# Cross-attention: the per-head merge as four transposes, the maximum row copied by ScalarE, the maximum tiles in another order

## The reference, cut to what matters

```
q = qdq(layernorm(x)) @ qdq(wq).T + bq          # 256 x 512
k, v = split(ctx @ wkv.T + bkv)                 # 4096 x 512 each
attn = softmax(q_h @ k_h.T / sqrt(32))          # for each of 16 heads: 256 x 4096
o_h  = attn @ v_h                               # 256 x 32
out  = qdq(concat(o_h)) @ qdq(wp).T + bp        # qdq: int8 rounding with a scale per row
```

## Time and profile before

| | us |
|---|---|
| three timed runs | 626.0, 627.62, 627.74 |
| median | 627.62 |
| the profiled execution | 625.34 |
| its span, first to last instruction | 623.5 |
| granted TensorE clock, mean | 0.997 of full speed |

### The profile page before, as it was taken

One profiled execution on the slowest core, in us unless ns is written; L12 is line 12 of the kernel. 1 busy time (PEld: TensorE's weight loads), 2 busy tenths in 40 slices (PEclk: granted clock), 3 DMA queues, 4 the chain that ended last, 5 costly groups with the idle time before them and its releaser, 6 DMA issues.

```text
span 623.5 us, 12623 instructions
## 1 busy us (share of the span) xinstructions
PE 603.5 (97%) x4455; PEld 482.0 (77%) x4456; DVE 369.4 (59%) x680; ACT 299.1 (48%) x424; POOL 228.4 (37%) x120
## 2 busy tenths in 40 slices
PE   8999999999999999999999999999899899999997
PEld 6877788888887677776777777776798789789996
DVE  3996530430434778887788788874764244376562
ACT  4444233233232555555555555555247678644451
POOL 2000200000002778887887888881100664410000
PEclk9999999999999999999999999999999899999999
DMA  8873644615639655556666555620032315145510
GB/s 292 310 238 121 188 171 160 202 67 161 208 102 280 172 152 151 147 155 158 159 158 157 147 147 147 157 83 2 1 136 69 136 67 202 69 159 199 187 63 34
DMA packets 29758, 92.19 MB, mean 148 GB/s; under 512 B 5472, under 2 KB 9568, under 8 KB 23008
## 3 DMA queue, kind: packets, MB, share of 16 engines
q1 hardware_dynamic: 28480, 89.67, 47.3%
q10 hardware_dynamic: 1248, 2.10, 0.9%
HBM read 65.02 MB, written 18.35 MB: 134 GB/s over the span
## 4 chain that ended last, share of the span: by engine, by line
PE 88%; DVE 4%; ACT 4%; issue 2%; POOL 1%; DMA 1%; POOLq 0%; SPq 0%; ACTq 0%; DVEq 0%
PE ps L340 16%; PE ps L341 16%; PE ps L342 16%; PE ps L1291 11%; PE ps L1388 10%; PE ps L1400 9%; PE ps L1414 4%; POOL p_sum L581 1%; PE ps L1374 1%; PE ps L1376 1%; ACT h_ring L772 1%; DMA f_ring<-stream 1%; PE ps L1273 1%; ACT probs L744 1%; PE ps L1364 1%
## 5 line engine op out<-in xcount | busy, mean ns | idle before, releaser
L700 ACT ACTIVATE p_ring<-ps 128x1024 f32<-128x1024 f32 x128 | 125.7, 1022 | 100.7 <-PE ps L1388 68.2
L961 DVE TENSOR_REDUCE m_part<-ps 128x1 f32<-128x512 f32 x240 | 150.5, 685 | 29.1 <-PE ps L1291 26.1
L581 POOL TENSOR_TENSOR p_sum<-p_sum,p_ring 128x1024 f32<-128x1024 f32 x60 | 142.8, 2380 | 9.1 <-ACT p_ring L700 4.8
L1291 PE MATMUL ps<-k_stack,q_max 96*128 96x512 f32 x240 | 86.7, 421 | 0.9 <-issue 0.6
L1388 PE MATMUL ps<-q_stack,k_stack 98*128 98x256 f32 x512 | 80.7, 286 | 0.2 <-ACT p_ring L700 0.2
L1388 PEld LDWEIGHTS ps<-q_stack,k_stack 98*128 98x128 f32 x512 | 74.8, 189 | 7.7 <-ACT p_ring L700 1.3
L1400 PE MATMUL ps<-p_ring,v_head 128*32 128x256 f32 x1024 | 71.6, 383 | 0.1
L1291 PEld LDWEIGHTS ps<-k_stack,q_max 96*128 96x128 f32 x240 | 40.9, 188 | 22.9 <-DVE m_part L961 12.7
L916 DVE SCALAR_TENSOR_TENSOR kl_buf<-ps,biases,kh_buf 128x512 fp32r<-128x512 f32 x32 | 23.6, 748 | 58.1 <-ACT kh_buf L661 57.8
L312 DVE TENSOR_TENSOR l_ring<-f_ring,h_ring 128x2048 fp32r<-128x2048 f32 x22 | 50.2, 2288 | 12.5 <-ACT h_ring L308 12.5
L340 PE MATMUL ps<-xt_h,h_ring 128*128 128x256 f32 x200 | 56.5, 282 | 0.0
(11 more groups left out here) (194 smaller groups left out, 1052.8 us busy)
## 6 DMA issues: line engine op xcount, KB each, us to landing
f_ring<-stream SPq DMA_DIRECT2D x29, 1024.0 KB, 4.9
k_stack<-kh_scratch SPq DMA_DIRECT2D x60, 256.0 KB, 4.6
kh_scratch<-kh_buf SPq DMA_DIRECT2D x32, 256.0 KB, 5.5
kl_scratch<-kl_buf SPq DMA_DIRECT2D x32, 256.0 KB, 5.9
v_head<-v_all SPq DMA_DIRECT2D x16, 512.0 KB, 3.0
k_stack<-kl_scratch SPq DMA_DIRECT2D x30, 256.0 KB, 4.2
v_all<-stream SPq DMA_DIRECT2D x4, 256.0 KB, 4.7
f_ring<-stream SPq DMA_DIRECT2D x4, 256.0 KB, 5.8
```

The lines of the kernel that those rows point to most:

```text
L581: nc.gpsimd.tensor_tensor(p_sum[:, p, :], p_ring[:, 0, :] if n == 0 else p_sum[:, p, :], p_ring[:, c % 4, :], ALU.add).then_inc(sums_done, 1)
L700: nc.scalar.activation(p_ring[:, c % 4, :], ps[:, 2 * (c % 2):2 * (c % 2) + 2, :].rearrange("p b n -> p (b n)"), ACT.Exp, scale=XSCALE).th ...
L961: nc.vector.reduce_max(m_part[:, j // NT, j % NT:j % NT + 1], maximum_bank(j), AX.X).then_inc(max_read, 1)
L1291: nc.tensor.matmul(maximum_bank(j), q_max[p][0:SPLIT_ROWS, at128(j % NT)], k_stack[p][0:SPLIT_ROWS, j // NT * D:(j // NT + 1) * D], start= ...
```

## The change

The merge becomes four fp32 transposes of `o_t` with the identity into bank 5 (numerators in its first half, denominators in the second). VectorE adds the four groups with two `tensor_reduce`, one of 8 denominators into `den`, one of 256 elements in PSUM into 64 elements of the same bank, then divides as before. The merge stands behind s6 and waits for the read of t13; t15 moves to bank 4, t1' waits for the read of t15, and the maximum rows, which use bank 5, wait until the outputs are written. VectorE's normalisation comes behind the negated maxima. ScalarE instead of VectorE copies the maximum row. The output maximum is taken once for heads 0 to 13, then for 14 and for 15. `pick` and its nine instructions on GpSimd go. The order on TensorE in one head, after:

```diff
+        def merge_bank():
+            return bank(5)
         def maximum_bank(j):
-            return bank((6, 4, 6)[j] if j < 3 else 5 if j == 15 else 4 + j % 3)
+            return bank((6, 4, 6)[j] if j < 3 else 4 + j % 3)
 # ScalarE
+            def maximum_row(h, p):
+                act.wait_ge(mrow_done, h + 1)
+                nc.scalar.copy(q_stack[p][SPLIT_ROWS:SPLIT_ROWS + MAX_ROWS, :], maximum_row_bank()).then_inc(mrow_ready, 1)
+            maximum_row(0, 0)
             exponentials(0, first=True)
-            with act.Fori(1, H - 1) as h:
-                exponentials(h)
+            maximum_row(1, 1)
+            with act.Fori(0, H // 2 - 1) as i:
+                exponentials(2 * i + 1)
+                maximum_row(2 * i + 2, 0)
+                exponentials(2 * i + 2)
+                maximum_row(2 * i + 3, 1)
 # VectorE
             def normalize_output(h):
                 dve.wait_ge(merge_done, h + 1)
-                order.step(nc.vector.reciprocal(r_den[:], bank(4).rearrange("p (t c) -> p t c", c=64)[:, 0:NT, DH]))
+                groups = merge_bank().rearrange("p (u g d) -> p u d g", u=2 * NT, d=DH)
+                added = merge_bank()[:, N:N + NT * DH].rearrange("p (t d) -> p t d", t=NT)
+                order.step(nc.vector.tensor_reduce(den[:], groups[:, NT:2 * NT, 0, :], axis=AX.X, op=ALU.add))
+                order.step(nc.vector.tensor_reduce(added, groups[:, 0:NT, :, :], axis=AX.X, op=ALU.add))
+                order.step(nc.vector.reciprocal(r_den[:], den[:]))
...
-                chunk_maxima(h + 1, 3, 15)
+                chunk_maxima(h + 1, 3, 16)
+                negate_maximum(h + 1)
                 if not first:
                     normalize_output(h - 1)
-                chunk_maxima(h + 1, 15, 16)
-                negate_maximum(h + 1)
-                if not first:
-                    output_maximum(h - 1)
                 if after:
-                    chunk_maxima(h + 2, 0, 2)
-                maximum_row(h + 1, 1 - p)
-                if after:
-                    chunk_maxima(h + 2, 2, 3)
+                    chunk_maxima(h + 2, 0, 3)
 # TensorE
             def maximum_rows(h):
                 pe.wait_ge(negm_ready, NT * h + NT)
+                wait(pe, o_done, NT * (h - 1))
...
             def merge(h, last_two=False):
                 pe.wait_ge(ot_evac, h + 1)
                 if not last_two:
-                    pe.wait_ge(max_read, 16 * (h + 2) + 13)
-                for t in range(NT):
-                    nc.tensor.matmul(bank(4)[:, 64 * t:64 * t + DH], o_t[:, at128(t)], pick[:, 0:DH],
-                                     start=True, stop=True)
-                    last = nc.tensor.matmul(bank(4)[:, 64 * t + DH:64 * t + DH + 1], o_t[:, at128(NT + t)],
-                                            pick[:, DH:DH + 1], start=True, stop=True)
+                    pe.wait_ge(max_read, 16 * (h + 2) + 14)
+                else:
+                    pe.wait_ge(o_done, NT * h)
+                for t in range(2 * NT):
+                    last = nc.tensor.transpose(merge_bank()[:, at128(t)], o_t[:, at128(t)], ident[:])
                 last.then_inc(merge_done, 1)
```

More of the change, by code:

```diff
@@ L136, in perceiver @@
         ident_b = sb("ident_b", [P, P], BF16)
-        pick = sb("pick", [P, DH + 1], F32)
         ones_col = sb("ones_col", [P, DH], F32)
@@ L549, in _ @@
             order.step(nc.gpsimd.memset(minus_half[:], -0.5))
-            for tile in (ident, ident_b, pick):
+            for tile in (ident, ident_b):
                 order.step(nc.gpsimd.memset(tile[:], 0.0))
@@ L555, in _ @@
                                         pattern=[[-1, P]], channel_multiplier=1).then_inc(consts_ready, 1)
-            for first in range(0, P, DH):
-                order.step(nc.gpsimd.affine_select(out=pick[:, 0:DH], in_=pick[:, 0:DH], compare_op=ALU.not_equal,
-                                                   fill=1.0, base=-first, pattern=[[-1, DH]], channel_multiplier=1))
-                order.step(nc.gpsimd.affine_select(out=pick[:, DH:DH + 1], in_=pick[:, DH:DH + 1],
-                                                   compare_op=ALU.not_equal, fill=1.0, base=-first,
-                                                   pattern=[[-1, 1]], channel_multiplier=1))
             nc.gpsimd.memset(ones_col[:], 1.0).then_inc(ones_set, 1)
@@ L1002, in normalize_output @@
+                added = merge_bank()[:, N:N + NT * DH].rearrange("p (t d) -> p t d", t=NT)
+                order.step(nc.vector.tensor_reduce(den[:], groups[:, NT:2 * NT, 0, :], axis=AX.X, op=ALU.add))
+                order.step(nc.vector.tensor_reduce(added, groups[:, 0:NT, :, :], axis=AX.X, op=ALU.add))
+                order.step(nc.vector.reciprocal(r_den[:], den[:]))
                 for t in range(NT):
-                    nc.vector.scalar_tensor_tensor(out=o_all[:, t, bass.ts(h, DH)], in0=bank(4)[:, 64 * t:64 * t + DH],
+                    nc.vector.scalar_tensor_tensor(out=o_all[:, t, bass.ts(h, DH)], in0=added[:, t, :],
@@ L1004, in normalize_output, with output_maximum @@
                                                    scalar=r_den[:, t:t + 1], in1=bv_row[:, bass.ts(h, DH)],
                                                    op0=ALU.mult, op1=ALU.add).then_inc(o_done, 1)
-            def output_maximum(h):
-                dve.wait_ge(o_done, NT * h + NT)
-                order.step(nc.vector.tensor_reduce(a_part[:, :, h], o_all[:, :, bass.ts(h, DH)], axis=AX.X,
+            def output_maximum(part, first, last):
+                dve.wait_ge(o_done, NT * last)
+                order.step(nc.vector.tensor_reduce(a_part[:, :, part], o_all[:, :, first * DH:last * DH], axis=AX.X,
@@ L1010, in output_maximum, with head @@
                                                    op=ALU.max, apply_absolute_value=True))
             negate_maximum(0)
-            chunk_maxima(1, 0, 2)
-            maximum_row(0, 0)
-            chunk_maxima(1, 2, 3)
-            def head(h, p, after=True):
+            chunk_maxima(1, 0, 3)
+            def head(h, after=True):
                 first = isinstance(h, int) and h == 0
-                chunk_maxima(h + 1, 3, 15)
+                chunk_maxima(h + 1, 3, 16)
+                negate_maximum(h + 1)
@@ L1034, in _ @@
             with dve.Fori(0, H // 2 - 2) as i:
-                order.enter(4, i, 8)
-                head(2 * i + 1, 1)
-                head(2 * i + 2, 0)
+                order.enter(4, i, 10)
+                head(2 * i + 1)
+                head(2 * i + 2)
                 order.leave(4, H // 2 - 2)
-            head(H - 3, 1)
-            head(H - 2, 0, after=False)
+            head(H - 3)
+            head(H - 2, after=False)
+            output_maximum(0, 0, H - 2)
             def add_last(n):
@@ L1285, in maxima @@
                     elif j == 1:
-                        wait(pe, o_done, NT * (h - 2))
+                        pe.wait_ge(max_read, 16 * h)
                     elif j == 4:
@@ L1362, in maximum_rows @@
                 pe.wait_ge(negm_ready, NT * h + NT)
+                wait(pe, o_done, NT * (h - 1))
                 for t in range(NT):
-                    last = nc.tensor.matmul(bank(5)[SPLIT_ROWS:SPLIT_ROWS + MAX_ROWS, at128(t)], neg_hl[:, t, :],
-                                            ident[:], start=True, stop=True)
+                    last = nc.tensor.matmul(maximum_row_bank()[:, at128(t)], neg_hl[:, t, :], ident[:],
+                                            start=True, stop=True)
                 last.then_inc(mrow_done, 1)
```

33 lines of the change are left out of this document (15 added, 18 removed).

## The result

The changed kernel takes 619.09 us (median of 4 runs, 618.13 to 619.6) against 626.81 us (4 runs, 625.21 to 627.74) of the kernel before on the same chip: 7.7 us less. The ratio on record is 0.9892 with an interval of 0.987 to 0.9913, a little nearer to one than the quotient of the two medians (0.9877); by the ratio it is 6.8 us less, 5.5 to 8.1. The forecast was 2.9 us less. The profiled execution takes 619.6 us with a span of 617.8, where that of before had 625.34 and 623.5: 5.7 us less, at the same mean granted clock of 0.997. I look for these 5.7 us, since both traces show them in full.

The account below looks back on a forecast made before the run. The key load was taken to set each loop head's start, with TensorE hardly earlier. -3.2 - 0.1 - 0.23 + 0.6 = -2.9 us on the 627.62 median gave 624.7 (60%), range 621.2 to 627.8.

Parts of the forecast that it names:

- -3.2 - 0.1 - 0.23 + 0.6: Cross-attention, in us: 14 heads with a key load, head 0, head 14, and the later end; together -2.9.
- From the profiled execution to the median: Whole kernel: the timed median, 627.62 us, lies 2.3 above the profiled execution, so -2.9 on it gives 624.7.
- The load sets t0': Loop: the next head's first maximum tile waits for the key load issued after score chunk s3, a 6.58 us path.
- The head at 14.56 us by t8's 0.23 us: Loop: maximum tile t8 behind score chunk s3 issues the key load 0.23 us earlier; head 14.56 instead of 14.79.
- Rival 1: Loop heads: the merge's gain arrives in full, each head 0.45 us shorter, 6.0 us in all, 621.6; chance 8%.
- Neither part without the other: TensorE from s3 to t0': the merge's saving only pays for moved tile t8, leaving a 0.26 us pause.
- Rival 4: TensorE's merge: transposes spaced by 275 ns make each head 0.17 us longer, 630.3 us in all; chance 5%.
- rival 3: VectorE's strided addition makes the normalisation late for the maximum rows; slower, 634 us at 1.8 us per addition; chance 7%.
- Rival 2: TensorE's loop: waits for banks and an exponential eat the saving, 0 to 0.1 us a head left, 626.9; chance 20%.
- The row copy: ScalarE copies the maximum row in 0.38 us, at most 0.59; nothing waits, with 0.2 us of cover.
- The end: Last head: VectorE's last sums start 0.3 us later and the last merge takes 0.3 more, together +0.6 us.
- The chance of faster, 0.66: Whole kernel: probability of a measurably faster result, beside 0.23 for same and 0.11 for slower; 1.9 us tells from no change.

Follow-up runs that it names:

- with rest 128: The changed kernel with wkv_h, wkv_l, kh_buf and kl_buf at 178048 and the other large tiles at rest 160: 619.53 us against 625.73, ratio 0.9902.

## Why the prediction was wrong, point by point

The number was wrong: 624.7 forecast with 621.2 to 627.8, and 619.09 measured. The 5.6 us between them are made up of two terms.

- *The sum ended at the edited code.* This is the step that failed: -3.2 - 0.1 - 0.23 + 0.6 was a sum over the parts of the diff, and the stage ahead of cross-attention stood in it at nothing without being named. It gave 2.9 us. The prediction even named `pick`, and costed only its instructions on GpSimd, not its bytes. That the places are the cause is shown from both sides: the changed code at the old places has 233.3 ns and loses the gain, the old code with 32 bytes more has 227.2 ns and 0.4% of the time. With the term, the sum for the profiled execution would have been 625.34 - 2.9 - 2.9 = 619.5, where 619.6 was measured.
- *From the profiled execution to the median.* I added 2.3 us, as three runs of before gave it. The changed kernel's median lies 0.5 us under its profiled execution, and beside the experiments the median of before was 625.39 to 626.81, not 627.62. That term was the scatter of three runs, 2.8 us of the miss, and it should have been in the range, not in the number. Two of the three, 627.62 and 627.74, lie where the executions with a mean granted clock of 0.995 lie (626.9 to 627.6), and the profiled one had 0.997; the clocks of those three are not on record. With both terms, 624.7 - 2.9 - 2.8 = 619.0.

The steps on the edited code:

- *The load sets t0'*: right. Landing to t0' 0.24 us in 12 of 14 heads, a landing of 4.7 us (4.6 forecast), and with the load shortened or issued earlier the head falls to 14.28 and 14.29 us (14.30 by the sum of the rows for TensorE alone).
- *The head at 14.56 us by t8's 0.23 us*: right, 14.55. Rival 1, the gain in full, would have had 14.34 and a t0' without a pause; it is false although the measured time is nearest to its 621.6. Whoever reads the median alone would take it for true.
- *Neither part without the other*: the text said that the merge only pays for t8. The two kernels with one part each show it, 0.03 and 0.09 us instead of 0.24; the first is not told from nothing, and with the second the head (14.700) is below all three kernels with the code before (14.785 to 14.834).
- *The merge*: four transposes in 0.35 us against 0.44 forecast. They are 0.11 us apart as forecast, but s7 starts only 0.03 us behind the last. Rival 4, a spacing of 275 ns, is false. The figure of the Trainium skill on the transpose ("TensorE: Matmul & The Clock Gate", "Part 4: PE-mode transpose"), some 275 ns in one kernel's context, agrees with the duration here (272 ns in the row of L1381), not with the spacing; the page gives it behind a figure for bf16, and these transposes are fp32.
- *VectorE*: the additions took 432 and 155 ns against 410 and 170. The stride of 32 elements costs 22 ns at most against the forecast line, so rival 3 is false: TensorE does not wait for VectorE at the maximum rows.
- *Rival 2, waits take the saved time*: no. The loop has its full forecast gain.
- *The row copy*: 365 ns against 380, and no product waits for it. ScalarE's slower start (0.1 to 0.2 us in the sum) does not show: the copy begins 0.04 us behind the product's end, as VectorE's did. Heads 0, 1 and 13 together have 0.84 where 0.8 was the sum, but by luck: head 0 gave 0.60 where 0.33 was forecast, and head 1 got 0.03 longer, behind a load that landed after 5.2 us where the kernel before had 4.0.
- *The end*: +0.64 against +0.6, the additions ahead of the last sums and the last reciprocal. In head 14 TensorE stands for GpSimd's sums, 1.04 us where it was 0.86, and the head gets -0.18 against -0.23: what was saved there disappears in that stand. That stand, and VectorE's last normalisation:

```profile
417.69 0.64 PE L1418 MATMUL ps<-p_sum,ones_col 128*32 128x256 f32 x8 [1.04 <-POOL p_sum L583]
```

```profile
429.79 0.17 DVE L1010 TENSOR_REDUCE den<-ps 128x2 f32<-128x8 f32 x1 [2.09 <-PE ps L1381]
429.99 0.43 DVE L1011 TENSOR_REDUCE ps<-ps 128x64 f32<-128x256 f32 x1
430.45 0.17 DVE L1012 RECIPROCAL r_den<-den 128x2 f32<-128x2 f32 x1
```

From the last merge (429.09) to the reciprocal 1.36 us, 1.09 in the earlier trace rows.

The chance of faster, 0.66, was on the right side, for a gain half of which had another cause.

What stays open: why the places matter. The runs tell when, not by what way. Nor is the direction in the feed-forward stage explained. Its 256-column products (`xt_h` or `ht_h` with the rings) start every 119.9 ns with tiles and rings both at rest 128 or both at 0, 119.8 with the tiles at 128 and the first two rings at 0, 118.3 with the tiles at 96, and 116.7 with them at 160 (rings at 128); the third ring moves with the tiles. So what is best for the 512 columns is the worst there. What it is worth in us shows once executions of the same clock are compared. From `out_q` to the end:

| granted clock from `out_q` to the end | 116.7 ns | 118.3 ns | 119.8 or 119.9 ns |
|---|---|---|---|
| full throughout | 182.2 to 182.3 (three kernels) | none | 183.2 (two) |
| 0.990 or 0.991 | 183.6, 183.7 | 184.5 to 184.8 (four) | 184.8 to 185.0 (three) |
| 0.982 | 185.0 | none | 186.1, 186.4 |

116.7 against 119.9 ns is worth 0.9 to 1.4 us, and each step down of the clock 1.0 to 1.9 us. What sets how often the clock falls, the runs don't tell.

## What to carry to other kernels

A diff that adds, removes or resizes a tile moves all tiles behind it, so compare the pace of stages that it does not edit, by products per stretch, before putting the whole time down to the edited lines; a pad that restores the old places tells the two apart. Where a start on an engine hangs on a transfer, find the instruction that releases the transfer: work moved from ahead of it to behind it counts at once, work merely saved behind it doesn't, and the two together can be worth more than their sum. Before two profiles are compared stage by stage, compare the granted clock of the stages. When a three-run median and the profiled execution differ by some tenths of a per cent, let the difference widen the range and keep it out of the forecast.

## What the runs showed of the hardware that I had not expected

- Products of 512 columns (fp32r, both operands in SBUF) start every 227.2 to 227.7 ns when the two operands' tiles start at the same rest by 256 bytes, and every 232.4 to 233.3 ns when the rests are 32, 64 or 128 apart, at the same granted clock of 1.00: 17 kernels of 17. Rests by 64 or by 128 don't decide it (192 and 0 against 128 are slow), and a period of 512 is excluded too: `wkv_h` started 177,792 bytes into the partition in the changed kernel and 256 bytes further with rest 128, and both had 227 ns.
- Products of 256 columns go the other way: 119.9 ns at the same rest, 118.3 and 116.7 at rests 96 and 160 against 128, but 119.8 at 128 against 0.
- Adding four groups with a stride of 32 elements straight from PSUM costs VectorE 432 ns for 256 elements into 64; a line through the contiguous rows of before (685 ns for 512, 0.21 us for 64) had given 410.
- The load in two pieces, the first issued two score chunks earlier, cost the loop nothing elsewhere: the head fell by the whole 0.26 us.
- Executions of one program differ by a stretch at 1.2 GHz (granted clock 0.50) behind `out_q`: with it the time from there to the end is 1.3 to 1.9 us longer at the same pace, and the time of the kernel before rose with it from 624.8 us on average at a mean clock of 1.000 (26 executions) to 626.0 at 0.997 (25) and 627.2 at 0.995 (five).
